# Two attention layers and an MLP on one core: value matmuls of a head's first unit one slot later, a norm chain in parts, and another order of transfers

## The reference

```
Q, K, V = multilora(x, ids, W, A, B)          # x @ W.T + (x @ A.T) @ B.T
Q, K = rope(Q), rope(K)                        # 16 heads of 32
attn = softmax(causal(Q K^T / sqrt(32)))
x = layernorm(x + multilora(attn V, ids, Wo, Ao, Bo))

h1 = rmsnorm(x, ln1_w); attn2 = attention(h1, Wq, Wk, Wv, Wo)
mod = 0.1 * tanh(attn2 @ A)
h = rmsnorm(x, ln2_w)
gate = silu(h @ W_in.T + mod * (h @ A) @ B)
out = layernorm(x + x + (gate * (h @ W_up.T)) @ W_down.T)
```

## Time and profile before

| | us |
|---|---|
| median of three runs (lowest, highest) | 2922.37 (2917.73, 2923.05) |
| the profiled execution | 2919.17 |
| its span | 2917.3 |
| PE busy | 2639.0 (90%) |
| DVE busy | 1580.4 (54%) |
| ACT busy | 1335.8 (46%) |
| POOL busy | 645.8 (22%) |

### The profile page before, as it was taken

How to read it: one execution, slowest core, us unless ns; L and a number is a source line. 1 busy time by engine, 2 the same in 40 slices (tenths; PEclk the granted TensorE clock), 3 DMA queues, 4 the chain that set the end, 5 groups by cost and what they waited for, 6 DMA issues and landing times. The chain is left out here.

```text
span 2917.3 us, 40940 instructions
## 1 busy us (share of the span) xinstructions
PE 2639.0 (90%) x13584; PEld 2029.4 (70%) x13584; DVE 1580.4 (54%) x4310; ACT 1335.8 (46%) x2755; POOL 645.8 (22%) x528
## 2 busy tenths in 40 slices
PE   5989988998748999899999884999999999999998
PEld 4767766776536666666666653888888888888886
DVE  3777777777635777776786763322222333333333
ACT  2776777767633666666666663211111221111111
POOL 5455555555321122222212111000000000000000
PEclk8999999999878999999999987999999999999999
DMA  5455555555625545455445534211111221111100
GB/s 139 96 140 135 141 121 136 132 131 118 153 85 125 120 101 137 109 111 132 112 107 130 109 64 143 88 45 45 44 44 44 77 91 46 45 45 44 44 29 29
DMA packets 173898, 276.44 MB, mean 95 GB/s; under 512 B 29204, under 2 KB 53524, under 8 KB 173076
## 3 DMA queue, kind: packets, MB, share of 16 engines
q1 hardware_dynamic: 170772, 260.58, 37.0%
q0 software_dynamic: 2304, 12.58, 1.3%
q10 hardware_dynamic: 640, 1.05, 0.1%
HBM read 97.04 MB, written 42.99 MB: 48 GB/s over the span
## 5 line engine op out<-in xcount | busy, mean ns | idle before, releaser
L2233 DVE TENSOR_TENSOR c_product<-c_up_ps,c_gate 128x512 f32<-128x512 f32 x128 | 88.6, 692 | 654.5 <-PE c_up_ps L2299 654.4
L2287 PE MATMUL c_gate_ps<-c_h_split,c_w_split 128*128 128x512 f32 x1536 | 381.2, 397 | 22.1 <-DVE c_w_split L2185 22.1
L2271 PE MATMUL c_down_ps<-c_w_split,c_product_split 128*128 128x512 f32 x1536 | 379.3, 396 | 0.0
L2299 PE MATMUL c_up_ps<-c_h_split,c_w_split 128*128 128x512 f32 x1536 | 378.2, 394 | 0.0
L2287 PEld LDWEIGHTS c_gate_ps<-c_h_split,c_w_split 128*128 128x128 f32 x1536 | 289.6, 189 | 94.4 <-issue 23.8
L2299 PEld LDWEIGHTS c_up_ps<-c_h_split,c_w_split 128*128 128x128 f32 x1536 | 288.1, 188 | 70.6
L2271 PEld LDWEIGHTS c_down_ps<-c_w_split,c_product_split 128*128 128x128 f32 x1536 | 288.4, 188 | 69.1
L2157 ACT ACTIVATE c_gate<-c_gate_ps 128x512 f32<-128x512 f32 x128 | 76.7, 599 | 494.2 <-PE c_gate_ps L2294 494.2
L280 ACT ACTIVATE b_prob_hi<-b_scores_t_ps 128x384 fp32r<-128x384 f32 (+1 forms) x384 | 201.1, 524 | 220.7 <-PE b_scores_t_ps L271 196.6
L288 DVE TENSOR_TENSOR a_prob_lo<-a_scores_t_ps,a_prob_hi 128x384 fp32r<-128x384 f32 (+1 forms) x384 | 225.7, 594 | 134.1 <-ACT a_scores_t_ps L281 132.5
L288 DVE TENSOR_TENSOR b_prob_lo<-b_scores_t_ps,b_prob_hi 128x384 fp32r<-128x384 f32 (+1 forms) x384 | 226.1, 594 | 124.1 <-ACT b_scores_t_ps L281 123.0
(11 more groups left out here) (206 smaller groups left out, 4776.7 us busy)
## 6 DMA issues: line engine op xcount, KB each, us to landing
a_q_stack<-a_q_split SPq DMA_DIRECT2D x192, 128.0 KB, 3.7
a_k_stack<-a_k_split SPq DMA_DIRECT2D x192, 128.0 KB, 3.7
b_q_stack<-b_q_split SPq DMA_DIRECT2D x192, 128.0 KB, 3.3
b_k_stack<-b_k_split SPq DMA_DIRECT2D x192, 128.0 KB, 3.6
c_h_stage<-h_t SPq DMA_DIRECT2D x16, 1024.0 KB, 6.2
c_res<-x SPq DMA_DIRECT2D x16, 1024.0 KB, 5.5
c_w_stage<-in_mlp_w POOLq DMA_DIRECT2D x16, 768.0 KB, 4.7
stage<-in_x_t SPq DMA_DIRECT2D x8, 1024.0 KB, 6.2
```

The lines of the kernel that those rows point to most:

```text
L2233: dve.tensor_tensor(product[:, bank, :], up_ps[:, bank, :], gate[:, bank, :], ALU.mult).then_inc(product_done, 1)
L2271: mm = pe.matmul(down_ps[:, t, :], product_split[:, kt % 2, a, t * P:t * P + P], w_split[:, w, kt, 2 * KC * P:], start=(kt == 0 and i == 0 ...
L2287: pe.matmul(gate_ps[:, bank, :], w_split[:, w, ft, c * 2 * P:c * 2 * P + P], h_split[run.pair][:, a, c, :], start=(c == 0 and w == 0 and a ...
L2299: mm = pe.matmul(up_ps[:, bank, :], w_split[:, w, ft, c * 2 * P + P:(c + 1) * 2 * P], h_split[run.pair][:, a, c, :], start=(c == 0 and w = ...
```

## The change

Value units: the first unit of a head (k % 3 == 0) was multiplied at the end of slot k+2, and is now in slot k+3 behind that slot's key-major scores, directly ahead of the second unit. The ring of the second layer gets a fourth buffer. In the first layer SP sends stack pair 0 between the two halves of the spread, gathers ahead of the load, and sends the adapter's B stack ahead of the gather; the adapter's low matmuls are shared 2, 3, 3, 4 over their slots instead of 3 each. In the second layer the same exchange of spread and stack is made in step 3 only, where POOL now merges ahead of its other work. The norm chain is cut in four parts around the low parts of slots 10 and 11.

```diff
+LOW_ITEMS = (range(0, 2), range(2, 5), range(5, 8), range(8, 12))
             def step(b, g):                      # first layer, SP
                 last = is_last(b)
+                first = isinstance(b, int) and b == 0 and g == 0
+                if g == 1 and not last:
+                    send_b(b + 1)
+                if not first:
+                    gather(*group(b, g, -1))
                 if g == 0 and not last:
                     load(b + 1)
-                first = isinstance(b, int) and b == 0 and g == 0
-                if not first:
-                    gather(*group(b, g, -1))
                 if g == 1 and not last:
-                    send_b(b + 1)
                     send_low(b + 1)
                 if not first:
-                    spread(*group(b, g, -1))
+                    spread_out(*group(b, g, -1))
                 if not (last and g >= 2):
                     stack_send(sp, at, *group(b, g, 2), 0)
                 if not first:
+                    spread_in(*group(b, g, -1))
                     store(*group(b, g, -1))
                 if not (last and g >= 2):
                     stack_send(sp, at, *group(b, g, 2), 1)
...
                     score_t_unit(pe, at, eye_bf, colmask, b, g, slot)   # PE, both layers
-                    if slot >= 2 and slot % 3 != 2:
+                    if slot >= 3 and slot % 3 == 0:
+                        value_needed(b, g, slot - 3)
+                        pv_unit(pe, at, b, g, slot - 3)
+                    if slot >= 3 and slot % 3 != 2:
                         value_needed(b, g, slot - 2)
                         pv_unit(pe, at, b, g, slot - 2)
-                    elif slot < 2 and not first:
-                        pv_unit(pe, at, *group(b, g, -1), UNITS - 2 + slot)
+                    elif slot == 0 and not first:
+                        pv_unit(pe, at, *group(b, g, -1), UNITS - 3)
+                        pv_unit(pe, at, *group(b, g, -1), UNITS - 2)
+                    elif slot == 1 and not first:
+                        pv_unit(pe, at, *group(b, g, -1), UNITS - 1)
...
-                        low(b + 1, share(3 * KC, LOW_SLOTS[1] - LOW_SLOTS[0], slot - LOW_SLOTS[0]))
+                        low(b + 1, LOW_ITEMS[slot - LOW_SLOTS[0]])
...
-                    if slot % 3 == 2:
-                        value_needed(b, g, slot - 2)
-                        pv_unit(pe, at, b, g, slot - 2)
...
-        at = Attention(nc, ctx, "b", RANK, 3, (1, 1, 2, 3))
+        at = Attention(nc, ctx, "b", RANK, 4, (1, 1, 2, 3))
...
                 if not first:                    # second layer, SP
-                    spread(*group(b, g, -1))
+                    spread_out(*group(b, g, -1))
+                if g < 3 and not first:
+                    spread_in(*group(b, g, -1))
...
                 if not (last and g >= 2):
                     stack_send(sp, at, *group(b, g, 2), 0)
+                if g == 3:
+                    spread_in(*group(b, g, -1))
...
+                    if not (isinstance(b, int) and b == 0 and g == 0):   # second layer, POOL
+                        merge(*group(b, g, -1))
                     if g == 3 and has(b, 2):
                         for c in range(KC):
                             attn_chunk(b + 2, c)
                         adapter(b + 2)
                     if not (isinstance(b, int) and b == 0 and g == 0):
-                        merge(*group(b, g, -1))
+                        weigh(*group(b, g, -1))
...
                 for slot in range(UNITS):        # second layer, DVE
+                    if g == 1 and slot == 10 and not last:
+                        variances(b + 1)
                     if slot > 0:
                         lo_unit(dve, at, b, g, slot - 1)
...
                         if slot == 10:
-                            norm_factors(b + 1)
+                            root_start(b + 1)
+                            root_round(b + 1, 0)
                         if slot == 11:
+                            for i in range(1, 3):
+                                root_round(b + 1, i)
                             normalise_tile(b + 1, 0)
                             normalise_tile(b + 1, 1)
```

More of the change, by code:

```diff
@@ L554, in spread, with spread_in @@
                 sp.dma_start(sums_hbm.rearrange("h (c n) -> (h c) n", c=TT), inverse[:, :]).then_inc(inverse_out, 16)
+            def spread_in(b, g):
+                n = number(b, g)
                 sp.wait_ge(inverse_out, n * 16 + 16)
@@ L1066, in _ @@
             batches(pe, body)
-            for k in range(UNITS - 2, UNITS):
+            for k in range(UNITS - 3, UNITS):
                 pv_unit(pe, at, BATCH - 1, GROUPS - 1, k)
@@ L1121, in rsqrt, with rsqrt_start @@
 def rsqrt(dve, step, done, out, x, t):
+    rsqrt_start(dve, step, done, out, x, t)
+    for i in range(3):
+        rsqrt_round(dve, step, done, out, x, t, i)
+def rsqrt_start(dve, step, done, out, x, t):
     dve.tensor_scalar(t.bitcast(I32), x.bitcast(I32), 1, None, ALU.logical_shift_right).then_inc(step, 1)
@@ L1125, in rsqrt, with rsqrt_round @@
     dve.tensor_scalar(out.bitcast(I32), t.bitcast(I32), -1.0, RSQRT_MAGIC, ALU.mult, ALU.add).then_inc(step, 1)
-    for i in range(3):
-        dve.wait_ge(step, done + 2 + 3 * i)
-        dve.tensor_tensor(t, out, out, ALU.mult).then_inc(step, 1)
-        dve.wait_ge(step, done + 3 + 3 * i)
-        dve.scalar_tensor_tensor(out=t, in0=t, scalar=-0.5, in1=x, op0=ALU.mult, op1=ALU.mult).then_inc(step, 1)
-        dve.wait_ge(step, done + 4 + 3 * i)
-        dve.scalar_tensor_tensor(out=out, in0=t, scalar=1.5, in1=out, op0=ALU.add, op1=ALU.mult).then_inc(step, 1)
+def rsqrt_round(dve, step, done, out, x, t, i):
+    dve.wait_ge(step, done + 2 + 3 * i)
+    dve.tensor_tensor(t, out, out, ALU.mult).then_inc(step, 1)
+    dve.wait_ge(step, done + 3 + 3 * i)
+    dve.scalar_tensor_tensor(out=t, in0=t, scalar=-0.5, in1=x, op0=ALU.mult, op1=ALU.mult).then_inc(step, 1)
+    dve.wait_ge(step, done + 4 + 3 * i)
+    dve.scalar_tensor_tensor(out=out, in0=t, scalar=1.5, in1=out, op0=ALU.add, op1=ALU.mult).then_inc(step, 1)
 RSQRT_STEPS = 11
@@ L1389, in merge, with weigh @@
                 pool.tensor_tensor(sum_hi[:, :], sum_hi[:, :], sum_lo[:, :], ALU.add).then_inc(merged, 1)
+            def weigh(b, g):
+                n = number(b, g)
                 pool.wait_ge(merged, n + 1)
@@ L1745, in _ @@
                 add_residual(0, t)
-            norm_factors(0)
+            variances(0)
+            root_start(0)
+            for i in range(3):
+                root_round(0, i)
             for t in range(TT):
```

25 lines of the change are left out of this document (16 added, 9 removed).

## The result

| | before | after |
|---|---|---|
| median, us (lowest, highest; runs) | 2922.71 (2917.73, 2923.9; 4) | 2949.97 (2947.84, 2952.98; 4) |
| the profiled execution, us | 2919.17 | 2947.84 |
| its span, us | 2917.3 | 2945.8 |
| mean granted clock | 0.961 | 0.952 |

The change makes the kernel slower: the ratio is 1.0097, 95% interval 1.008 to 1.0115, or 27 us. The forecast was 2944, in a range of 2900 to 2980.

The account below looks back on a forecast made before the run. PE was taken to set the pace, with SP's queue loop as long as the step where ACT waits. First layer +33, value order -4, norm chain -6, second queue -1: +22, median 2944 us, range 2900 to 2980.

Parts of the forecast that it names:

- The loop in the queue: First layer, SP's queue: the loop through store, gather and ACT's copy grows to 23.6 us a step, 28.7 with adapter stack.
- +33: First layer's total: 29 us in seven batches, 6 in the last batch, -2 for the very first step.
- The 0.6 us taken off for shorter sends: First layer, SP's queue: both stack sends take 3.76 us instead of 4.39, so 0.6 off the loop.
- its 0.3 for the value order: First layer: ACT gets key-major scores up to 0.6 us earlier; half of that, 0.3, comes off each step's loop.
- The broadcast behind six sends: First layer, SP's queue: from broadcast to multiply taken as 3.69 us even behind six 128 KB sends.
- the slow end: First layer: landing at 5.9 us makes a step 2.2 longer, 29 steps, +64; the range's text used 2944 + 31.
- rival 1: Faster: first layer's loop stays shorter than PE's step; 26 us less there, 11 in the second, 2885; chance 0.20.
- The stack waits: First layer: stack 0 starts 1.6 us earlier, so most of PE's 14.1 us in six batches vanishes.
- The second layer: Second layer: value unit later -4, norm chain -6, queue and POOL order -1 us.
- The terms -4 and -6: Second layer: value unit later shortens copy waits, -4 us; norm chain brings low parts earlier, -6 us in seven batches.
- Rival 2: No change: only the adapter stack's step binds, +3 us a batch, the rest gives it back; 2922; chance 0.10.
- Rival 3: Slower by the clock: PE's longer waits bring stretches at 1.2 GHz, 3 to 4 us a batch more; 2970; chance 0.12.

Follow-up runs that it names:

- k10: The changed kernel with the first layer's store moved behind stack pair 1's six sends, the broadcast still behind pair 0; 2923.45 us, ratio 0.9995.
- k3: The kernel before with only the value unit one slot later in both layers and the second layer's fourth buffer; 2896.3 us, ratio 0.9904.
- k7: The changed kernel with the first layer's queue and the shares of the adapter's low matmuls as before the change; 2896.28 us, ratio 0.9898.
- k1: The changed kernel with the first layer's broadcast back in front of stack pair 0's sends; 2885.94 us, ratio 0.9863.

## Why the prediction was right, and where its sizes were off

The mechanism was right, and the total (+22 forecast, +28.7 between the profiles) is closer than its parts by luck: the first layer lost 12.6 us more than forecast, the second gained 8.7 more, and 2.8 came from elsewhere.

**The loop in the queue.** Right, and it decides: SP waits at the store (4.6 us each, about 4 forecast), the gather goes later, ACT waits in every step but two (1.8 us in the mean, 2 to 4 forecast). The means of six batches from the timelines of SP, POOL and ACT after, plain steps and the one with the adapter stack, beside the forecast (the terms, then the loop):

| us | way out to broadcast | to multiply | to store | to last gather | to copy | to next way out | loop |
|---|---|---|---|---|---|---|---|
| forecast, plain | 4.8 | 3.7 | 1.4 | 5.75 | 4.4 | 4.4 | 24.5 less 0.9 = 23.6 |
| after, plain | 4.60 | 3.95 | 1.32 | 5.89 | 4.02 | 4.26 | 24.04 |
| after, adapter | 4.32 | 4.37 | 1.32 | 7.81 | 3.98 | 7.29 | 29.09 (forecast 28.7) |

A batch is 3 x 24.04 + 29.09 = 101.2 us against 99.5, and in seven batches that is 12 us: all but a little of the difference between +33 and the measured +45.6. Three terms of a plain step were too small. The 0.6 us taken off for shorter sends was there by 0.2 only (4.60 against 4.8), the multiply came 0.25 later, and the way from the copy to the next way out had its 0.3 for the value order (4.09 in undisturbed steps) but lost 0.17 in the mean to the clock, which the sum had at nothing (see the rivals). The copy, 0.4 sooner than taken, gave part of this back.

**The broadcast behind six sends.** I took 3.69 us from its own row. Issue to landing, view by source line, before and after:

```profile
DMA to landing us min/median/max: 2.9/3.6/3.8
```

```profile
DMA to landing us min/median/max: 3.0/3.9/4.5
```

The queue ahead costs the broadcast some 0.3 us. The rule of the Trainium skill ("DMA: Bandwidth & Descriptors", Queues, rings and completion order) that I weighed points the right way, and its size here is a seventh of the way to the slow end that I had kept open (5.9). For the store it is larger. Behind six sends it lands in 3.5 us in the median (before, and k10), and in after, with nothing right ahead, in 2.0.

Two statements on the range don't hold. The 64 us of the slow end (2.2 us in 29 steps) come on top of the +33 and would give 3008, not 2944 + 31. And 2900 is not half way to rival 1 but three quarters.

**The stack waits.** I let most of the 14.1 us vanish; 12.4 remain. All these waits were for pair 0 before and are for pair 1 after: pair 0 lands early now, but pair 1 starts 10.07 us behind the way out instead of 7.11.

**The second layer.** -11 forecast, -19.7 in the profile, and -13 to -15 in five other profiles of the same code. The value order was priced at 4 from the copy waits alone; k3 shows 13, mostly from waits for low parts, which I had given wholly to the norm chain. The low parts at the chain moved as forecast. DVE after:

```profile
1237.34 0.68 DVE L288 TENSOR_TENSOR b_prob_lo<-b_scores_t_ps,b_prob_hi 128x512 fp32r<-128x512 f32 x1
1238.82 0.55 DVE L288 TENSOR_TENSOR b_prob_lo<-b_scores_t_ps,b_prob_hi 128x384 fp32r<-128x384 f32 x1
```

From the first to the second it is 1.48 us instead of 3.93, 2.45 less where 2.3 was forecast. The terms -4 and -6 add only in part, as told with k7.

**The value order in the first layer.** "A loop in the queue that binds swallows both" says too much. The 0.3 us a step that the forecast had itself put into the loop were there, some 9 us in 31 steps by my estimate. Where the loop is free the value order is worth 12.4 us (k3), and the forecast had no such number.

**The rivals.** Rival 1 (loop shorter than PE's step) didn't come by landing times. Its price of 2885 us is what k1 measured (2885.9) with the queue's order put back, but in other parts: k1's profile has 18.3 us less in the first layer and 13.0 in the second, where the rival had 26 and 11. Rival 2 needed a plain loop of 22 us, and it was 24. Rival 3, the clock, came in part. After, busy time by stretch, and PE's timeline at the fall:

```profile
206.50:212.50 6.00, 5.13 (x18) 3.96 (x19) 3.60 (x10) 4.11 (x9) 3.75 (x3) 0.50 0.00 0
```

```profile
207.37 0.66 PE L305 MATMUL a_pv_ps<-a_prob_hi,a_value 128*65 128x512 f32 x1 [2.81 <-ACT a_pv_raw L317]
```

PE stands 2.81 us at the copy, and within this wait (at 206.3) the clock falls to its lower level, 1.2 GHz. In six batches the clock withheld (what is missing to full speed, times its duration) is worth 27.3 us after, in 11 falls, and 5.1 before, in three; PE is busy 18.8 us more.

What of this reaches the time can be read in the loop, in the term that runs through PE: from the first head's copy to the next way out. Two plain steps after, this stretch alone, with a low clock and without (the same columns):

```profile
335.47:340.43 4.96, 4.22 (x17) 3.25 (x18) 2.70 (x9) 3.16 (x7) 3.73 (x3) 0.66 0.02 5
360.73:364.82 4.09, 3.35 (x21) 2.75 (x22) 2.69 (x9) 3.76 (x9) 3.76 (x3) 1.00 0.00 0
```

The 24 steps fall into groups by it. In the 14 plain steps whose stretch has no low clock it takes 4.08 to 4.10 us; in three with a long one 4.96, and in one with a short one 4.52. In the adapter's step it takes 7.43 in four with a long one and 6.99 and 7.03 in two with a shorter one, against 6.56 in k10, where there is none. By my estimate this adds up to 7.4 us in six batches, 1.2 a batch, where the rival had 3 to 4. So it is about a fifth of the 36.5 us that six batches lost. The loop doesn't need it to bind: in k10 the clock fell four times in six batches. What it costs elsewhere was not tested; as ACT's copy waits for the gather in 29 steps, PE's slower work ahead of that copy should not count.

## What to carry to other kernels

Before moving sends past each other in a queue, follow the queue around: which later send waits for an engine that waits for the moved one. Work that stood between a broadcast and the store that needs its result was free there. Put ahead, it is on the path: the store went 9.63 us behind the way out instead of 6.42, and the queue stood idle behind the broadcast. The cost has a knee where the loop reaches the step of the busiest engine, so three sends cost a fifth of what six did. Try the parts of such a change apart, since one moved line hid a gain of 38 us.

Delaying the consumer by a slot and speeding the producer can remove the same microseconds. Such gains should not be added before a run has shown that they add.

## What the hardware showed that I had not expected

- A 256 KB broadcast behind six 128 KB sends landed 0.3 us later in the median (3.9 against 3.6 us); with six sends issued right behind it, it was some 0.3 us later still (4.4 against 4.06 us from issue to multiply in the means of k10 and after).
- A store of 256 KB landed 3.5 us after its issue (median; 2.2 to 3.8 in k10) with six sends right ahead of it, and 2.0 with nothing right ahead (after). In k10 this landing is exposed, since the gather waits for it.
- In six batches after the clock fell 11 times to 0.50, for 3 to 7 us each; in six batches before, three times. Two of them (at 206 and 309) begin within a wait of PE of 2.8 us at the copy.
- A step bound by a queue pays for TensorE's lower clock only in part: 4.96 us instead of 4.09 from the copy to the next way out, and about 7 us in six batches with 27.3 us of clock withheld (an estimate from these stretches).
